# Attention value products gathered behind the two-bank score groups, and a hinted back edge for TensorE's loops

## The chip, the cores and the metric

One core of a Trainium2 chip. The metric is device time in microseconds for one execution of the whole program.

## The reference

One layer: attention with 16 heads of 16 features over 4096 rows of 256 features, a layer norm, an int8 feed-forward product and a second layer norm. Only the attention matters here. In short:

```python
query = qt_c + qt_r                      # [1, 16, 4096, 16]
key = kt_c + kt_r
value = heads(ct_kv @ Wu_v_w + Wu_v_b)
attn = jnp.einsum('bhqd,bhkd->bhqk', query, key) / scale
attn = jax.nn.softmax(attn, axis=-1)
out = jnp.einsum('bhqk,bhkd->bhqd', attn, value)
...
x = _layernorm(x + attention(x), axis=-1)
x = _layernorm(x + ffn(x), axis=-1)
```

## The kernel before

**Units.** A unit is one head with one half (2048) of the queries. There are 32 of them, done in 16 *pairs* (`PAIRS`), and a pair is one turn of the loop body on every engine. For a unit there are 32 tiles of 128 keys (`KT`) and 4 blocks of 512 queries (`QB`). A score block is a 128x512 product that fills one PSUM bank. Keys are split in two halves that lie in different partitions (rows 0 to 48 and 64 to 112), and blocks from different halves that stand next to each other run at the same time.

**Steps.** ScalarE makes the exponentials of 29 of the 32 key tiles, in 78 groups a pair (`NG`): even groups take four banks (0 to 3), odd ones two (4 and 5). Only group 38 is an even group of two. I call them exp 0 to exp 77. TensorE's body (`pair`) is one *step* for each group: wait for exp `s`, whose banks are then free; score group `s + 2` into them; at four steps in 13 one more score block in bank 6, for VectorE, which makes the exponentials of key tiles 15, 30 and 31 by bit operations and a polynomial (a *D block* below); and then the value products that stand in `VALUES[s]`. A D block waits until VectorE has read the one before it.

**Value products.** `values` multiplies the exponentials of one key tile with its values, for all four query blocks: four fp32 matmuls into four column strips of bank 7 (`OT`), which the trace shows as eight records. I call this a *set*. There are 64 in a pair, in a fixed order. After the last set of a unit VectorE copies bank 7 and normalises (`norm`, lines 770 to 786); the first set of the next unit waits for the copy. In VectorE's order the whole of `norm` stands ahead of its reading of the next D block.

**Where the sets stand.** `make_values` gives each set the first step, not before its exponentials are ready, that has no set yet. What is left over lands in step 77, so that step 77 has two sets.

**Loops.** TensorE runs pairs 0 to 8 in one loop, pair 9 written out (it also multiplies attention by the output weights, `project_step`), pairs 10 to 14 in a second loop, and pair 15 written out. So 12 of the 15 boundaries between pairs on TensorE are taken branches (8 in the first loop, 4 in the second), and at 3 of them (8 to 9, 9 to 10, 14 to 15) the code runs straight on. The other engines have loops of their own, which the change does not touch.

Of the kernel before, what the change touches and what calls it, by code (L numbers as in the profile page):

```python
# [19 lines left out]
PAIRS = NT // 2  # L20
# [33 lines left out]
NG = len(GROUPS)  # L54
# [15 lines left out]
def make_values():  # L70

    ready = []
    for g, (par, blocks) in enumerate(GROUPS):
        ready += [(g, par, kt) for kt, j in blocks if [b for b in ORDER if b[0] == kt][-1] == (kt, j)]
    for c in range(CYCLES):
        ready.append((STEPS_A_CYCLE * c + 6, c // len(BY_VECTOR), BY_VECTOR[c % len(BY_VECTOR)]))
    at = [[] for _ in range(NG)]
    earliest = 3
    for par in range(2):
        step = earliest  # L80
        for g, _, kt in sorted(r for r in ready if r[1] == par):
            step = max(step, g)
            at[min(step, NG - 1)].append((par, kt))
            step += 1
        earliest = step + 2
    return at


VALUES = make_values()
VALUE_ORDER = [v for at in VALUES for v in at]  # L90
assert [par for par, _ in VALUE_ORDER] == [0] * KT + [1] * KT
# [25 lines left out]
PROJECT_PAIR = 9  # L117
# [44 lines left out]
def build(nc, xT_d, x_d, w_d, bias_d, rows_d, tab_d, sel_d, ident_d, w8_d, out_d,  # L162
# [11 lines left out]
    with ctx:  # L174
# [323 lines left out]
        def attention_tensor(pe, a):  # L498
# [51 lines left out]
            def pair(i, more=True, project=False):  # L550
                for s in range(NG):
                    c, at = divmod(s, STEPS_A_CYCLE)

                    pe.wait_ge(a.exp, NG * i + s + 1)
                    if s + 2 < NG:
                        scores(s + 2)
                    elif more:
                        scores(s + 2 - NG)
                    if at in BLOCK_STEPS and (more or c + AHEAD < CYCLES):
                        n = QB * c + BLOCK_STEPS.index(at)  # L560
                        if project and n and (n - 1) % 3 == 0:
                            pe.wait_ge(a.added, (n - 1) // 3 + 1)
                        cycle_block(i, c, BLOCK_STEPS.index(at))
                    if project and at - 1 in BLOCK_STEPS:
                        n = QB * c + BLOCK_STEPS.index(at - 1)
                        if n % 3 == 0:
                            if n == 0:
                                pe.wait_ge(a.heads[0], 16 * 2)
                                pe.wait_ge(a.yb, KT)
                            project_step(n // 3)  # L570
                    for par, kt in VALUES[s]:
                        values(i, par, kt)
# [10 lines left out]
                    block(n, 0, kt, j)  # L583

            bias_out()
            with pe.Fori(0, PROJECT_PAIR) as i:
                pair(i)
            pair(PROJECT_PAIR, project=True)
            with pe.Fori(PROJECT_PAIR + 1, PAIRS - 1) as i:
                pair(i)  # L590
            pair(PAIRS - 1, more=False)

        def bias_out():

            for k in range(2):
                last = nc.tensor.matmul(PS[:, OT * CH:OT * CH + D], bv_wide[:, k, :],
                                        w[:, W_O + k * D:W_O + (k + 1) * D], start=k == 0, stop=k == 1)
            last.then_inc(s_bo, 1)
# [411 lines left out]
        def _(pe):  # L1010
# [64 lines left out]
            pe.wait_ge(s_dve, DONE - STEPS)  # L1075
            lengths("k", 0, 0)
            make_values(0, 8, (0, 0, 0, 0, 1, 2, 3, 4))

            pe.wait_ge(s_dve, DONE - STEPS + 5)
            pe.wait_ge(s_ev, E0 + 8)  # L1080
            lengths("k", 1, 4)

            pe.wait_ge(s_dve, DONE + 1)
            make_values(8, 12, (8, 8, 8, 8))

            pe.wait_ge(s_dve, DONE + 2)
# [13 lines left out]
            pe.wait_ge(s_sums, 1)  # L1100

            attention_tensor(pe, fast)


# [588 lines left out]
```

## Time and profile before

| what | value |
|---|---|
| device time, median of 3 runs | 2161.41 us (2157.86 to 2163.83) |
| profiled execution: its own time | 2160.25 us |
| profiled execution: its span | 2158.4 us |
| TensorE matmul busy | 1889.0 us (88%) |
| ScalarE busy | 1819.0 us (84%) |
| VectorE busy | 1612.8 us (75%) |
| mean granted TensorE clock | 0.958 |

The busy time is that of the whole span. Busy time of TensorE's weight loads is kept apart and overlaps with the matmuls. The clock is given as a share of full speed (2.4 GHz).

### The profile page before, as it was taken

How to read it: one execution, taken by the hardware profiler on the slowest of the kernel's cores; microseconds unless marked ns; L12 is line 12 of the kernel's file. 1: busy time of each engine (PE TensorE's matmuls, PEld its weight loads, DVE VectorE, ACT ScalarE, POOL GpSimd, SP SyncE). 2: the span in 40 equal slices, each digit the busy share in tenths (PEclk: the TensorE clock that was granted, in tenths of full speed). 3: DMA queues.
4: the chain of work that ended last, by engine and by line, in shares of the span. 5: the costliest groups of instructions: out<-in, count | busy, mean ns of one | idle time of the engine just before them, and what ended most of it. 6: DMA issues, size and time to landing. Idle time of an engine off the chain costs nothing.

```text
span 2158.4 us, 35517 instructions
## 1 busy us (share of the span) xinstructions
PE 1889.0 (88%) x13009; PEld 430.8 (20%) x13009; DVE 1612.8 (75%) x1514; ACT 1819.0 (84%) x1418; POOL 166.8 (8%) x129
## 2 busy tenths in 40 slices
PE   8957989898998989898989899898989989899975
PEld 3431111111111111111111122111111111111134
DVE  3648878777777777787777767887897778777838
ACT  4445989898998989898989977899989989898955
POOL 5725200000000000000000000000030000000002
PEclk9987999999999999999999999999999999999997
DMA  5652111110011111111111101111110101111012
GB/s 184 205 184 85 23 24 23 24 21 18 14 19 22 23 24 23 24 23 24 23 29 49 19 12 23 23 23 24 23 23 11 21 17 23 24 23 23 3 38 79
DMA packets 165495, 81.87 MB, mean 38 GB/s; under 512 B 130204, under 2 KB 146716, under 8 KB 164856
## 3 DMA queue, kind: packets, MB, share of 16 engines
q1 hardware_dynamic: 164024, 78.11, 14.0%
q8 instruction: 139, 2.28, 0.5%
q10 hardware_dynamic: 1312, 1.32, 0.2%
q14 instruction: 20, 0.16, 0.0%
HBM read 48.83 MB, written 29.23 MB: 36 GB/s over the span
## 4 chain that ended last, share of the span: by engine, by line
PE 68%; ACT 15%; issue 8%; DVE 5%; DMA 1%; SPq 1%; ACTq 0%; POOL 0%; DVEq 0%; POOLq 0%
PE PS L539 39%; PE PS L502 24%; ACT arena L762 15%; PE PS L1017 4%; PE PS L604 1%; DVE bn L692 1%; DMA Qst<-parts_or_sums 1%; DVE arena L816 1%; DVE arena L793 0%; DVE arena L1621 0%; DVE arena L746 0%; SPq L429 0%; DVE arena L749 0%; DVE parts_or_sums L1439 0%; DMA arena<-xT_dram 0%
## 5 line engine op out<-in xcount | busy, mean ns | idle before, releaser
L762 ACT ACTIVATE arena<-PS 128x2048 f32<-128x2048 f32 (+1 forms) x1248 | 1712.5, 1443 | 211.6 <-PE PS L502 202.1
L539 PE MATMUL PS<-arena,Vh 128*32 128x512 f32 x8192 | 1106.6, 614 | 0.5 <-ACT arena L762 0.5
L502 PE MATMUL PS<-Qst,Kst 49*128 49x512 f16 x4096 | 722.1, 393 | 207.3 <-ACT arena L762 145.7
L816 DVE SCALAR_TENSOR_TENSOR arena<-arena 128x2048 f32<-128x2048 f32 x288 | 660.4, 2293 | 0.2
L793 DVE TENSOR_SCALAR arena<-PS 128x512 int32<-128x512 f32 x384 | 265.2, 691 | 409.6 <-PE PS L502 398.7
L502 PEld LDWEIGHTS PS<-Qst,Kst 49*128 49x128 f16 x4096 | 156.2, 94 | 1205.6 <-ACT arena L762 772.0
L539 PEld LDWEIGHTS PS<-arena,Vh 128*32 128x32 f32 x8192 | 163.8, 108 | 378.9 <-issue 377.1
L812 DVE SCALAR_TENSOR_TENSOR arena<-arena 128x2048 f32<-128x2048 f32 x96 | 220.5, 2297 | 0.0
L800 DVE TENSOR_SCALAR arena<-arena 128x2048 int32<-128x2048 int32 x96 | 118.7, 1237 | 9.5
L738 POOL TENSOR_TENSOR ctkv<-arena,rows 128x256 f32<-128x256 f32 x16 | 21.2, 1362 | 1343.0 <-DVE arena L719 1343.0
L802 DVE TENSOR_SCALAR arena<-arena 128x2048 int32<-128x2048 int32 x96 | 118.7, 1237 | 0.0
L1017 PE MATMUL PS<-arena,w 128*128 128x512 f32 x192 | 90.3, 619 | 10.8 <-DMA bias<-biases_dram 6.8
L1220 ACT ACTIVATE arena<-PS,bias 128x512 f32<-128x512 f32 x56 | 38.4, 687 | 42.9 <-PE PS L1017 36.4
L738 POOL TENSOR_TENSOR arena<-arena,rows 128x256 f32<-128x256 f32 x16 | 11.1, 728 | 504.7 <-ACT arena L724 504.7
L1017 PEld LDWEIGHTS PS<-arena,w 128*128 128x128 f32 x192 | 38.0, 199 | 59.7 <-issue 52.6
L734 POOL TENSOR_TENSOR arena<-arena,rows 128x256 f32<-128x256 f32 x32 | 46.6, 1493 | 38.8 <-DVE rows L1458 38.8
L1427 DVE TENSOR_TENSOR arena<-arena 128x512 f32<-128x512 f32 x16 | 17.3, 1086 | 42.7 <-POOL arena L1342 40.2
L770 DVE COPY parts_or_sums<-PS 128x512 f32<-128x512 f32 x32 | 22.1, 691 | 33.5 <-PE PS L539 33.2
L1339 POOL TENSOR_TENSOR arena<-arena 32x512 f32<-32x512 f32 x16 | 26.2, 1638 | 39.4 <-DMA arena<-arena 39.4
L1439 DVE TENSOR_TENSOR parts_or_sums<-arena,parts_or_sums 128x1024 f16<-128x1024 f32 x16 | 27.4, 1751 | 0.0
L1340 POOL TENSOR_TENSOR arena<-arena 32x512 f32<-32x512 f32 x16 | 26.6, 1663 | 0.0
L604 PE MATMUL PS<-w,ctkv 128*128 128x256 f32 x64 | 19.1, 450 | 6.5 <-DVE arena L793 6.5
(104 smaller groups left out, 491.8 us busy)
## 6 DMA issues: line engine op xcount, KB each, us to landing
Kst<-k_halves SPq DMA_DIRECT2D x64, 128.0 KB
Qst<-q_halves SPq DMA_DIRECT2D x64, 128.0 KB
Vh<-head_values SPq DMA_DIRECT2D x30, 256.0 KB, 6.8
arena<-xT_dram SPq DMA_DIRECT2D x8, 512.0 KB, 5.3
k_halves<-parts_or_sums SPq DMA_DIRECT2D x16, 256.0 KB, 2.4
k_whole<-arena SPq DMA_DIRECT2D x8, 512.0 KB, 3.4
q_halves<-parts_or_sums SPq DMA_DIRECT2D x16, 256.0 KB, 3.4
q_whole<-arena SPq DMA_DIRECT2D x8, 512.0 KB, 4.3
```

Source lines behind the costliest of these rows:

```text
L502: return nc.tensor.matmul(out, Kst[par][low:low + HK + 1, at:at + 128], Qst[par][low:low + HK + 1, j * CH:(j + 1) * CH], start=True, stop= ...
L539: last = nc.tensor.matmul(PS[32 * j:32 * j + 32, OT * CH:(OT + 1) * CH], Vh[par][:, kt, :], moving, start=kt == first, stop=kt == last_kt)
L604: last = nc.tensor.matmul(out, heads_out(t // TH, c, t % TH * 128, 128), w[:, W_O + c * D:W_O + (c + 1) * D], start=c == 0 and starts, sto ...
L734: nc.gpsimd.tensor_tensor(Y[:, t, :], Y[:, t, :], bo, ALU.add).then_inc(s, 1)
L762: nc.scalar.activation(P[:, at * CH:(at + k) * CH], bank(SLOT_BANKS[g % 2][0], k), ACT.Exp, scale=EXP_SCALE).then_inc(a.exp, 1)
L793: nc.vector.tensor_scalar(bits[:, j * CH:(j + 1) * CH].bitcast(int32), bank(D_BANK), LOWEST, TO_BITS, ALU.max, ALU.mult).then_inc(b_bits, 1)
L800: nc.vector.tensor_scalar(mantissa.bitcast(int32), bits.bitcast(int32), 0x007FFFFF, 0x3F800000, ALU.bitwise_and, ALU.bitwise_or).then_inc( ...
L802: nc.vector.tensor_scalar(power.bitcast(int32), bits.bitcast(int32), 0x7F800000, 0x40000000, ALU.bitwise_and, ALU.bitwise_xor).then_inc(b_ ...
L812: nc.vector.scalar_tensor_tensor(out=t, in0=mantissa, scalar=POLY[3], in1=mantissa, op0=ALU.add, op1=ALU.mult).then_inc(b_poly, 1)
L816: last = nc.vector.scalar_tensor_tensor(out=t, in0=t, scalar=POLY[3 - j], in1=power if j == 3 else mantissa, op0=ALU.add, op1=ALU.mult)
L1017: last = nc.tensor.matmul(bank(out_bank), l, r, start=k == 0, stop=k == len(lhsT) - 1)
L1220: nc.scalar.activation(dst[e], bank(e), ACT.Identity, bias=bs[e], scale=scales[e]).then_inc(s_ev, 1)
```

## The change

`make_values` moves each set on to the next odd step, and lets an odd step take two sets; the last step takes what is left. TensorE's two loops get a hint for their closing branch, which stands as an instruction of its own at the head of the body. The order of the sets, all products and all waits stay.

```diff
@@ -80,8 +80,9 @@
         step = earliest
         for g, _, kt in sorted(r for r in ready if r[1] == par):
             step = max(step, g)
+            while step < NG - 1 and (step % 2 == 0 or len(at[step]) == 2):
+                step += 1
             at[min(step, NG - 1)].append((par, kt))
-            step += 1
         earliest = step + 2
     return at
 
@@ -583,10 +584,10 @@
             bias_out()
-            with pe.Fori(0, PROJECT_PAIR) as i:
+            with nc.Fori(0, PROJECT_PAIR, engines=(pe.engine,), hint_back_edge=True) as i:
                 pair(i)
             pair(PROJECT_PAIR, project=True)
-            with pe.Fori(PROJECT_PAIR + 1, PAIRS - 1) as i:
+            with nc.Fori(PROJECT_PAIR + 1, PAIRS - 1, engines=(pe.engine,), hint_back_edge=True) as i:
                 pair(i)
```

On TensorE, the order of the instructions in steps 3 to 7 of a pair, before (L502 is a score block, L539 the matmuls of a set, L554 and L513 the register steps of the waits for an exp and for VectorE):

```order
L502 MATMUL PS<-Qst,Kst 128x512
L529 ISA
L530 ISA
L539 MATMUL PS<-arena,Vh 32x512 x4
L554 REGISTER_ALU
L502 MATMUL PS<-Qst,Kst 128x512 x4
L539 MATMUL PS<-arena,Vh 32x512 x4
L554 REGISTER_ALU
L502 MATMUL PS<-Qst,Kst 128x512 x2
L539 MATMUL PS<-arena,Vh 32x512 x4
L554 REGISTER_ALU
L502 MATMUL PS<-Qst,Kst 128x512 x4
```

The same place after the change (all line numbers are one higher):

```order
L503 MATMUL PS<-Qst,Kst 128x512
L530 ISA
L531 ISA
L540 MATMUL PS<-arena,Vh 32x512 x8
L555 REGISTER_ALU
L503 MATMUL PS<-Qst,Kst 128x512 x4
L555 REGISTER_ALU
L503 MATMUL PS<-Qst,Kst 128x512 x2
L540 MATMUL PS<-arena,Vh 32x512 x8
L555 REGISTER_ALU
L503 MATMUL PS<-Qst,Kst 128x512 x4
```

The D block of step 3 has two sets behind it in place of one, and the four-bank scores of step 4 have none.

On TensorE, the end of a pair (steps 75 to 77) and the closing branch, before:

```order
L502 MATMUL PS<-Qst,Kst 128x512 x2
L554 REGISTER_ALU
L502 MATMUL PS<-Qst,Kst 128x512 x4
L539 MATMUL PS<-arena,Vh 32x512 x4
L554 REGISTER_ALU
L502 MATMUL PS<-Qst,Kst 128x512 x2
L539 MATMUL PS<-arena,Vh 32x512 x8
L586 REGISTER_ALU
L586 COMPARE_AND_BRANCH
```

After:

```order
L503 MATMUL PS<-Qst,Kst 128x512 x2
L540 MATMUL PS<-arena,Vh 32x512 x4
L555 REGISTER_ALU
L503 MATMUL PS<-Qst,Kst 128x512 x4
L555 REGISTER_ALU
L503 MATMUL PS<-Qst,Kst 128x512 x2
L540 MATMUL PS<-arena,Vh 32x512 x12
L587 REGISTER_ALU
L587 COMPARE_AND_BRANCH
```

Step 76 loses its set, and step 77 has three. The hint stands at the other end of the body, ahead of step 0:

```order
L587 UNCONDITIONAL_BRANCH
L587 BRANCH_PREFETCH_HINT
L587 ISA
L503 MATMUL PS<-Qst,Kst 128x512 x4
L514 ISA
L503 MATMUL PS<-Qst,Kst 128x512
```

In a pair, 63 steps had a set before; 35 have one after: 27 with two, 7 with one, and step 77 with three. The last set of the pair's first unit stands in step 39 (before: 38).

## Rows read from the trace of the kernel before

**Rows 1.** The page: busy time by engine, and the costliest groups
```profile
PE 1889.0 (88%) x13009; PEld 430.8 (20%) x13009; DVE 1612.8 (75%) x1514; ACT 1819.0 (84%) x1418; POOL 166.8 (8%) x129
...
L762 ACT ACTIVATE arena<-PS 128x2048 f32<-128x2048 f32 (+1 forms) x1248 | 1712.5, 1443 | 211.6 <-PE PS L502 202.1
...
L502 PE MATMUL PS<-Qst,Kst 49*128 49x512 f16 x4096 | 722.1, 393 | 207.3 <-ACT arena L762 145.7
```

**Rows 2.** Timeline, middle of a pair: start us, us, instructions [idle before]
```profile
599.85 1.87 ACT L762 ACTIVATE arena<-PS 128x2048 f32<-128x2048 f32 x1
601.61 1.03 ACT L762 ACTIVATE arena<-PS 128x1024 f32<-128x1024 f32 x1
...
602.06 0.61 PE L502 MATMUL PS<-Qst,Kst 49*128 49x512 f16 x4
602.60 1.07 PE L539 MATMUL PS<-arena,Vh 128*32 128x512 f32 x8
603.60 0.39 PE L502 MATMUL PS<-Qst,Kst 49*128 49x512 f16 x2
603.91 1.07 PE L539 MATMUL PS<-arena,Vh 128*32 128x512 f32 x8
604.91 0.82 PE L502 MATMUL PS<-Qst,Kst 49*128 49x512 f16 x5
```

**Rows 3.** Timeline, boundary of pairs 14 and 15, without a branch
```profile
1955.00 5.48 ACT L762 ACTIVATE arena<-PS 128x2048 f32<-128x2048 f32 x4 [0.27 <-PE PS L502]
1958.78 1.92 PE L539 MATMUL PS<-arena,Vh 128*32 128x512 f32 x16
1960.64 1.04 PE L502 MATMUL PS<-Qst,Kst 49*128 49x512 f16 x7
1960.77 0.69 DVE L770 COPY parts_or_sums<-PS 128x512 f32<-128x512 f32 x1 [0.46 <-PE PS L539]
1961.36 5.48 ACT L762 ACTIVATE arena<-PS 128x2048 f32<-128x2048 f32 x4 [0.89 <-PE PS L502]
1963.30 0.60 PE L502 MATMUL PS<-Qst,Kst 49*128 49x512 f16 x4 [1.62 <-ACT arena L762]
1965.30 0.60 PE L502 MATMUL PS<-Qst,Kst 49*128 49x512 f16 x1 [0.70 <-DVE arena L793]
1965.83 1.93 PE L539 MATMUL PS<-arena,Vh 128*32 128x512 f32 x8
1968.77 1.88 ACT L762 ACTIVATE arena<-PS 128x2048 f32<-128x2048 f32 x1 [1.93 <-PE PS L502]
1979.31 5.64 ACT L762 ACTIVATE arena<-PS 128x2048 f32<-128x2048 f32 x4 [0.20 <-PE PS L502]
```

**Rows 4.** Timeline, boundaries with the taken branch
```profile
534.48 1.37 PE L502 MATMUL PS<-Qst,Kst 49*128 49x512 f16 x7 [1.93 <-issue]
...
643.66 5.48 ACT L762 ACTIVATE arena<-PS 128x2048 f32<-128x2048 f32 x4 [0.27 <-PE PS L502]
651.73 1.04 PE L502 MATMUL PS<-Qst,Kst 49*128 49x512 f16 x7 [2.36 <-issue]
667.70 4.73 ACT L762 ACTIVATE arena<-PS 128x2048 f32<-128x2048 f32 x3 [0.20 <-PE PS L502]
...
760.42 5.48 ACT L762 ACTIVATE arena<-PS 128x2048 f32<-128x2048 f32 x4 [0.27 <-PE PS L502]
785.69 4.73 ACT L762 ACTIVATE arena<-PS 128x2048 f32<-128x2048 f32 x3 [0.20 <-PE PS L502]
...
886.73 1.89 PE L502 MATMUL PS<-Qst,Kst 49*128 49x512 f16 x7 [2.59 <-issue]
```

**Rows 5.** Stretches at the first and last boundary: us, busy time by engine, clock, DMA share, GB/s
```profile
301.00:305.00 4.00, 2.81 (x12) 0.51 (x15) 3.38 (x3) 3.70 (x3) 0.00 (x0) 0.50 0.35 89
...
1960.50:1964.50 4.00, 2.07 (x17) 0.51 (x13) 3.33 (x7) 3.14 (x3) 0.00 (x0) 1.00 0.22 73
1965.50:1971.50 6.00, 6.00 (x27) 0.84 (x30) 4.74 (x3) 3.54 (x4) 0.00 (x0) 0.50 0.62 95
```

## The prediction

> **What bounds the kernel now.** I read the page first. ScalarE and TensorE are both near 85% busy, and in the attention each waits for the other: the exponentials had 211.6 us of idle time ahead of them, nearly all ended by score blocks, and the score blocks had 207.3 us, most of it ended by the exponentials [rows 1]. So neither engine's sum is the limit. What counts is the ring: exp `s` frees its banks, scores `s + 2` fill them, exp `s + 2` can start.
>
> Then the timeline of a pair's middle. A four-bank exp is followed by the next after 1.76 us (601.61 - 599.85), and is itself 1.87 us long; a two-bank one is 1.03 us long [rows 2]. Four exps in a row take 5.48 us, of which the last two take 1.76 + 1.03 = 2.79, so an undisturbed double step takes ScalarE 2.69 us and the two-bank exp 0.93 of it [rows 2, 3]. TensorE: four-bank scores hold it for 0.54 us before the next set starts (602.06 to 602.60), two-bank ones 0.31, and a lone D block adds 0.21 (five blocks take 0.82, four 0.61), and a set 1.00 before the next scores (602.60 to 603.60) [rows 2].
>
> Then the boundary of two pairs, with z the start of exp 76. With the taken branch, TensorE stands still for 2.36 us on nothing the trace shows but issue (1.93 to 2.59 us at the 11 boundaries where it is named so) [rows 4]. From z to the start of exp 12 of the next pair it is 24.04 us (643.66 to 667.70) in one case and 25.27 in another (760.42 to 785.69) [rows 4]. Undisturbed, these 14 groups would be seven double steps, 7 x 2.69 = 18.8. From exp 12 on to the next exp 76 it is 92.72 us (667.70 to 760.42) [rows 4], against 31 x 1.76 + 33 x 0.93 = 85.3 undisturbed. So a pair loses about 5.2 to 6.4 us at its boundary and 7.4 us inside.
>
> The view that matters most is the boundary *without* a branch [rows 3]. There TensorE resumes at once (1960.64), and ScalarE waits only 0.89 us. But z to exp 12 is 24.31 us (1955.00 to 1979.31), as long as with the branch. VectorE can begin `norm` only at 1960.77, and reads the D block of step 0 only behind it; so the D block of step 3 waits until 1965.30, 4.53 us later, with the set and the four-bank scores of step 4 queued behind it, and ScalarE starves 1.93 us before exp 6 [rows 3]. TensorE, which had idled 1.62 us and then 0.70 us, is moreover at a granted clock of 0.50, the lower level of 1.2 GHz, over 1965.5 to 1971.5, after 1.00 up to 1964.5 (it fell at each of the 15 boundaries, the first of them at 301) [rows 5]; a set takes 1.93 us there [rows 3] in place of 1.07 [rows 2]. With the branch, these waits lie under the standstill.
>
> **The change, part by part.**
>
> *1. Sets by two.* Two sets back to back take 1.86 us until the next scores (1958.78 to 1960.64) [rows 3] where two apart take 2.00, so the second costs 0.87. Counting what is spared around the moved scores too: TensorE's double step with one set in each step is 0.54 + 1.00 + 0.31 + 1.00 = 2.85; with both sets behind the two-bank scores it is 0.43 (scores run straight on) + 0.31 + 1.86 = 2.60, or 0.25 less. In a pair 63 - 35 = 28 such changes go.
>
> What is it worth? Four-bank scores now wait for both sets, and these for the two-bank exp. The ring is: end of a two-bank exp, 0.05 until scores start, 0.31 of scores, 1.86 of sets, 0.65 from the start of four-bank scores to their exp, 1.76 to the next two-bank exp, 1.03 of it: 5.66 us for two double steps, 2.83 each. (0.05: I take the smallest wait that fits; 0.65 is 602.06 plus 0.61 plus hand-over.) Before, it was TensorE's own 2.85. So 0.02 is gained where 0.25 is spared: TensorE gets idle time, ScalarE little. D blocks in even steps (half of 24) become hidden behind the wait for the exp; those in odd steps still cost 0.22. Where double steps have fewer than two sets ScalarE is the limit in both versions.
>
> Laid out step by step with these durations from exp 12 to exp 76, the losses of ScalarE are, before: 4 x 0.14, 8 x 0.35, 7 x 0.24 and 1.54 around the two-bank groups 38 and 39, sum 6.6 (the trace has 7.4); after: 8 x 0.27, 4 x 0.22, 4 x 0.48, 3 x 0.05 and 1.44, sum 6.6. So inside a pair I take **0.0**. By averages (27 double steps with two sets; D blocks cost 0.62 x 0.22 each before, 0.31 x 0.22 after) it would be 27 x (2.99 - 2.90) = 2.4 us a pair less, or 39 us in all; that bounds it below.
>
> The last set of the pair's first unit moves from step 38 to 39, so `norm` and the D block of step 42 come about 1.2 us later. Nothing hangs on that block at once: steps 42 and 43 have no sets now. I take 0.
>
> *2. Three sets in step 77.* From z: exp 77 ends at 2.79, scores by 3.15, three sets 1.00 + 0.87 + 0.87 = 2.74, next scores at 5.9 (before, without a branch: 1960.64 - 1955.00 = 5.64 [rows 3]). So `norm` and all behind it come 0.25 us later.
>
> *3. The hint.* It takes away at most the standstill of 2.36 us [rows 4]; how much, no row shows: from 0 to all of it. I take all but a few tenths, since the target is known a whole pair ahead; the hint itself is one instruction in a step where TensorE then waits 1.62 us for ScalarE [rows 3]. A gap g of up to 0.5 us costs nothing, as the D block of step 3 is later anyway.
>
> The Trainium skill (Runtime: NRT & Kernel Launch, Instruction fetch mechanics) says that a taken branch to code outside the fetched pages stalls for the fetch. The trace agrees so far as the standstill stands at 12 branches and not at the straight boundaries.
>
> *4. The boundary then.* It becomes that of [rows 3], with three sets. From z: exp 2 at 5.9 + 0.65 = 6.55; D block of step 3 at 10.30 + 0.2 = 10.5 (1965.30 - 1955.00 = 10.30 [rows 3]); two sets from 10.8; scores of step 4 at 12.7, exp 6 at 13.35, 1.4 later than ScalarE could; exp 8 without loss at 16.05; exp 10 at 19.0; exp 12 at **21.7**. That holds at full clock. If the clock falls there as in [rows 5], two sets take 1.7 us more, scores 0.4, and exp 8 and exp 10 come late as well: exp 12 at **24.5**. Against the mean of the two branch cases, 24.65, a boundary gains 2.9 or 0.2.
>
> Does the clock fall? It fell at all 15 boundaries before, but at 12 of them after the standstill that goes now. Of the three straight ones, the one in [rows 3] had the idle times that I expect here (1.62 and 0.70), and there it fell. So neither end is excluded, and I take half: 1.4 us for each of 12 boundaries. The three straight ones stay.
>
> **Sum.** 12 x 1.4 = 17 us off 2160.25, the profiled execution's own time (span 2158.4 and 1.85 around it; 1.2 below the median of the runs): 2143 us.
>
> **The rivals.**
>
> *A, likeliest (0.48): the standstill goes and the clock holds at some or all boundaries.* 2118 (12 x 2.9 and some at the straight ones) to 2153; 2143 in the middle.
>
> *B (0.24): the standstill goes, nothing is gained.* `norm`, the D block of step 3 and the fallen clock take it all back, as in [rows 3]. 12 x 0.2: 2154 to 2162. For it: z to exp 12 without a branch equals that with one. Against it: the one sample.
>
> *C (0.10): the hint does nothing.* Then TensorE resumes at 8.07 from z as before (651.73 - 643.66 [rows 4]), the third set partly under the fetch, but step 3 has two sets at the low clock: 0.3 to 1.0 us more at 12 boundaries, 2164 to 2172.
>
> *D, slower (0.10): the second set of a step costs more than 0.87.* The 1.86 us stands in one kind of place only, step 77. If the second set cost 1.00, the ring would be 5.79 for two double steps: 27 x 0.065 = 1.8 us a pair, 28 us in all, and with A's 17 that is 2171. From 0.08 us more on a second set it outweighs A.
>
> *E (0.08): TensorE's sum does count.* If the scores of an even step could start well before they are needed, 28 x 0.25 = 7 us a pair would go, up to the 7.4 that a pair loses inside: 16 x 7 = 112 us, 2048. Against it: the ring of 5.66 us. The Trainium skill (TensorEngine Tiling (Array Packing), Key Properties) says that a change of tiling mode drains TensorE, which is what each change between scores (row tiles) and sets (column strips) is; by it alone the change would be worth this rival's time. The trace agrees with a cost, 0.25 us by the rows above.
>
> **The numbers.** Faster by over 0.3% (about what a measurement here tells from no change) means below 2155: A nearly whole and E, some of D's small end: 0.57. Within 0.3%: B and the edges of A and C, 0.27. Slower: 0.16. The range 2116 to 2166 takes A, B and a part of C, about 8 in 10.
>
> **What the profile after should show.** The "issue" gap before the scores of step 0 below 0.5 us at 12 boundaries (C wrong); ScalarE waiting about 1.1 us at exp 2; TensorE waiting for VectorE at step 3's D block; z to exp 12 between 21.7 and 24.5, and the clock low at fewer than 15 boundaries (A) or at all (B). Inside a pair, exp 12 to exp 76 at 92 to 93 us (E: below 88; D: above 94), with waits of about 0.27 us ahead of every second four-bank exp, and 16 records of a set pair in 1.92 us. TensorE's busy time falls while its waits for ScalarE grow. The prediction is wrong if the time inside a pair changes by over 1 us, or if the clock behaves alike at all boundaries.

## The result, and the profile after

The changed kernel takes 2239.16 us (median of 4 runs, 2237.22 to 2241.12) against 2162.03 us beside it: a ratio of 1.036, 95% interval 1.0341 to 1.0378. It is slower by 77 us where 17 to 19 us of gain were forecast. Two executions in what follows, one of e7 (3469.74 us) and one of the kernel before beside e5 to e8 (3475.03 us), ran in a slow state of the chip and count in no ratio.

The page of the kernel after, with the rows that answer to [rows 1], and the queue of instruction fetches:

```profile
PE 1920.4 (86%) x13009; PEld 500.5 (22%) x13009; DVE 1609.7 (72%) x1514; ACT 1813.0 (81%) x1418; POOL 166.8 (7%) x129
...
q8 instruction: 31, 0.51, 0.1%
...
L763 ACT ACTIVATE arena<-PS 128x2048 f32<-128x2048 f32 (+1 forms) x1248 | 1706.6, 1442 | 297.4 <-PE PS L503 294.6
...
L503 PE MATMUL PS<-Qst,Kst 49*128 49x512 f16 x4096 | 712.5, 402 | 255.2 <-ACT arena L763 199.0
```

ScalarE's idle time ahead of the exponentials has grown from 211.6 to 297.4 us, by 85.8; with the 5.9 us less that the exponentials themselves take (1712.5 to 1706.6) that is 80 of the 81 us by which the span grew (2158.4 to 2239.3). TensorE's idle time ahead of the scores grew from 207.3 to 255.2 us. The sets are the same work, and TensorE is busy 31 us longer with it: it ran slower. The mean granted clock over the span fell from 0.958 to 0.914.

The boundary of two pairs in the timeline after, with z, the start of exp 76, at 664.09:

```profile
664.09 5.48 ACT L763 ACTIVATE arena<-PS 128x2048 f32<-128x2048 f32 x4 [0.26 <-PE PS L503]
...
667.26 2.78 PE L540 MATMUL PS<-arena,Vh 128*32 128x512 f32 x24
...
669.97 1.04 PE L503 MATMUL PS<-Qst,Kst 49*128 49x512 f16 x7
...
670.70 5.48 ACT L763 ACTIVATE arena<-PS 128x2048 f32<-128x2048 f32 x4 [1.13 <-PE PS L503]
...
674.98 0.60 PE L503 MATMUL PS<-Qst,Kst 49*128 49x512 f16 x1 [1.05 <-DVE arena L794]
675.52 3.64 PE L540 MATMUL PS<-arena,Vh 128*32 128x512 f32 x16
...
680.16 2.79 ACT L763 ACTIVATE arena<-PS 128x2048 f32<-128x2048 f32 x2 [3.99 <-PE PS L503]
...
688.64 1.89 ACT L763 ACTIVATE arena<-PS 128x2048 f32<-128x2048 f32 x1
...
786.97 5.48 ACT L763 ACTIVATE arena<-PS 128x2048 f32<-128x2048 f32 x4 [0.26 <-PE PS L503]
```

The standstill of [rows 4] is gone: the scores of step 0 follow the three sets at once (669.97). The D block of step 3 waits 1.05 us for VectorE, its two sets take 3.64 us at the low clock, and ScalarE starves 3.99 us before exp 6. From z to exp 12 (688.64, read in a narrower stretch, which is why it stands alone) it is 24.55 us, against 24.04 and 25.27 in [rows 4]. So the boundary cost what it did before: added over all 15 boundaries of the two traces, z to exp 12 is 372.5 us before and 372.5 after.

The loss is inside the pair. The next exp 76 begins at 786.97, so exp 12 to exp 76 takes 98.33 us where it took 92.72 [rows 4]. Added over the 16 pairs it is 1579 us in place of 1500. The place around steps 41 to 45 in the timeline after (at 615.38 step 42 has brought no set, step 43 none, and step 44 begins):

```profile
610.94 1.92 PE L540 MATMUL PS<-arena,Vh 128*32 128x512 f32 x16
612.80 0.61 PE L503 MATMUL PS<-Qst,Kst 49*128 49x512 f16 x4
613.45 5.48 ACT L763 ACTIVATE arena<-PS 128x2048 f32<-128x2048 f32 x4 [0.19 <-PE PS L503]
613.62 0.60 PE L503 MATMUL PS<-Qst,Kst 49*128 49x512 f16 x3 [0.22 <-DVE arena L794]
615.38 0.63 PE L503 MATMUL PS<-Qst,Kst 49*128 49x512 f16 x4 [1.15 <-ACT arena L763]
616.29 1.04 PE L503 MATMUL PS<-Qst,Kst 49*128 49x512 f16 x3 [0.29 <-ACT arena L763]
617.26 3.64 PE L540 MATMUL PS<-arena,Vh 128*32 128x512 f32 x16
...
621.91 2.79 ACT L763 ACTIVATE arena<-PS 128x2048 f32<-128x2048 f32 x2 [2.98 <-PE PS L503]
```

Two sets take 3.64 us there and 1.92 before it. Between 612.80 and 617.26 TensorE has only scores, and waits for ScalarE in between. The idle times behind steps 17 and 67 are of the same kind (1.47 us, then 0.31; and 1.84):

```profile
576.44 0.60 PE L503 MATMUL PS<-Qst,Kst 49*128 49x512 f16 x4 [1.47 <-ACT arena L763]
...
653.02 1.57 PE L503 MATMUL PS<-Qst,Kst 49*128 49x512 f16 x7 [1.84 <-ACT arena L763]
```

The stretches of the same trace, behind the odd steps 17, 43 and 67, which have no set, and at the boundary (columns as in [rows 5]):

```profile
577.90:581.00 3.10, 3.10 (x17) 0.58 (x16) 2.89 (x2) 2.09 (x2) 0.00 (x0) 0.56 0.00 0
617.00:621.90 4.90, 4.90 (x23) 0.88 (x22) 4.36 (x3) 1.93 (x2) 0.00 (x0) 0.50 0.49 60
654.00:656.50 2.50, 2.50 (x15) 0.63 (x18) 2.29 (x2) 2.50 (x2) 0.00 (x0) 0.50 0.00 0
675.00:680.00 5.00, 5.00 (x23) 0.95 (x23) 4.92 (x3) 1.17 (x2) 0.00 (x0) 0.50 0.70 96
```

TensorE is at or near the low level of 1.2 GHz at four places in a pair, where it was at one. ScalarE's waits behind them, in every pair of the first loop: 2.05 us (before exp 22), 2.98 us (exp 48), 1.56 us (exp 72). Each is the first exp whose scores stand behind the slow sets.

### The profile page after: what moved, and what is told of

It reads as the page before. It is cut to its first block, busy times and chain, and to the rows that moved or that the text cites. A ratio compares the mean times of both kernels' runs of the same rounds, so it can differ in the third digit from the quotient of the medians.

```text
span 2239.3 us, 35532 instructions
## 1 busy us (share of the span) xinstructions
PE 1920.4 (86%) x13009; PEld 500.5 (22%) x13009; DVE 1609.7 (72%) x1514; ACT 1813.0 (81%) x1418; POOL 166.8 (7%) x129
## 4 chain that ended last, share of the span: by engine, by line
PE 52%; issue 21%; ACT 14%; DVE 9%; DMA 1%; SPq 1%; ACTq 1%; POOL 0%; DVEq 0%; POOLq 0%
PE PS L540 31%; PE PS L503 16%; ACT arena L763 13%; PE PS L1018 4%; PE PS L605 1%; DVE arena L794 1%; DVE parts_or_sums L778 1%; DVE parts_or_sums L773 1%; DVE parts_or_sums L771 1%; DVE bn L693 1%; DMA Qst<-parts_or_sums 1%; DVE arena L1622 0%; DVE arena L817 0%; ACTq L757 0%; DVE sum_inv L776 0%
## 5 line engine op out<-in xcount | busy, mean ns | idle before, releaser
L763 ACT ACTIVATE arena<-PS 128x2048 f32<-128x2048 f32 (+1 forms) x1248 | 1706.6, 1442 | 297.4 <-PE PS L503 294.6
L540 PE MATMUL PS<-arena,Vh 128*32 128x512 f32 x8192 | 1083.2, 645 | 1.6 <-ACT arena L763 1.6
L503 PE MATMUL PS<-Qst,Kst 49*128 49x512 f16 x4096 | 712.5, 402 | 255.2 <-ACT arena L763 199.0
L503 PEld LDWEIGHTS PS<-Qst,Kst 49*128 49x128 f16 x4096 | 168.9, 95 | 1079.8 <-ACT arena L763 895.3
L540 PEld LDWEIGHTS PS<-arena,Vh 128*32 128x32 f32 x8192 | 219.5, 115 | 515.0 <-issue 509.3
```

The costliest lines, as they stand in the source:

```text
L503: return nc.tensor.matmul(out, Kst[par][low:low + HK + 1, at:at + 128], Qst[par][low:low + HK + 1, j * CH:(j + 1) * CH], start=True, stop= ...
L540: last = nc.tensor.matmul(PS[32 * j:32 * j + 32, OT * CH:(OT + 1) * CH], Vh[par][:, kt, :], moving, start=kt == first, stop=kt == last_kt)
L763: nc.scalar.activation(P[:, at * CH:(at + k) * CH], bank(SLOT_BANKS[g % 2][0], k), ACT.Exp, scale=EXP_SCALE).then_inc(a.exp, 1)
```

## The experiments

Each ratio is against the kernel before, run beside that experiment.

Theory 1, formed from these rows: sets by two leave stretches without any set, longest where an odd step is empty; TensorE's clock falls there, and the two sets behind the stretch then run at half speed, with the four-bank scores, and so ScalarE, behind them. The rivals: the hint disturbs TensorE (theory 2), or the ring through two sets is long at any clock (theory 3).

**e1: the hint alone.** The kernel before with the loops of the change:

```diff
-            with pe.Fori(0, PROJECT_PAIR) as i:
+            with nc.Fori(0, PROJECT_PAIR, engines=(pe.engine,), hint_back_edge=True) as i:
```

> The hint alone, sets where they stood before. Theory 1 (the loss of the change is the low clock in stretches of a pair in which TensorE has no sets; the branch's standstill only covered a wait for VectorE): 2150 to 2165 us, the clock low once a pair, z to exp 12 about 24.3 us at every boundary as at the straight one, and 92 to 93 us from exp 12 to exp 76. Theory 2 (the hint itself disturbs TensorE's instruction supply and costs what was lost): 2200 to 2240 us. If the clock holds at some boundaries once the standstill is gone: 2115 to 2150.

2141.63 us, ratio 0.9921 (0.9904 to 0.9937), so about 17 us faster. Theory 2 falls. The boundary in its timeline, with z at 640.91:

```profile
640.91 5.48 ACT L762 ACTIVATE arena<-PS 128x2048 f32<-128x2048 f32 x4 [0.27 <-PE PS L502]
...
646.56 1.04 PE L502 MATMUL PS<-Qst,Kst 49*128 49x512 f16 x7
...
651.57 0.39 PE L502 MATMUL PS<-Qst,Kst 49*128 49x512 f16 x1 [1.05 <-DVE arena L793]
...
654.32 1.88 ACT L762 ACTIVATE arena<-PS 128x2048 f32<-128x2048 f32 x1 [1.56 <-PE PS L502]
...
661.12 2.79 ACT L762 ACTIVATE arena<-PS 128x2048 f32<-128x2048 f32 x2 [0.27 <-PE PS L502]
664.11 5.64 ACT L762 ACTIVATE arena<-PS 128x2048 f32<-128x2048 f32 x4 [0.20 <-PE PS L502]
...
756.83 5.48 ACT L762 ACTIVATE arena<-PS 128x2048 f32<-128x2048 f32 x4 [0.27 <-PE PS L502]
```

z to exp 12 is 23.20 us, 0.8 to 2.1 below the two of [rows 4]. Exp 12 to exp 76 is 92.72 us, the same to the hundredth as before. My expectation of about 24.3 at every boundary missed: the standstill of 2.4 us is covered by the wait for VectorE only in part, and the clock is low for a shorter time at eight of the twelve hinted boundaries (before: at two). Added up, the hinted boundaries are 15 us shorter. Another 3 us come from the straight boundary of pairs 14 and 15, which the hint does not touch: the clock held there this time (z to exp 12 is 21.25 us, 24.31 in [rows 3]).

**e2: the sets by two alone**, loops closed as before:

```diff
-            with nc.Fori(0, PROJECT_PAIR, engines=(pe.engine,), hint_back_edge=True) as i:
+            with pe.Fori(0, PROJECT_PAIR) as i:
```

> The sets by two alone, loops closed as before. Theory 1: 2235 to 2255 us, the clock low four times a pair, at the boundary and behind the odd steps without a set (17, 43, 67). Theory 2: back at about 2160. The branch's standstill should be there again, under 2.6 us, shorter if the third set of step 77 hides a part of the fetch.

2223.92 us, ratio 1.0308 (1.0291 to 1.0326), mean clock 0.933. So the loss comes with the sets. The time lies below the range that I gave, and 15 us below the whole change, though the standstill is back. The low clock fell into fewer places: its share of the span, (1 - clock) x 2, is 0.134, or 298 us, against 0.172, or 385 us. The trace splits the difference to the whole change: without the hint the 15 boundaries are 14 us longer (387 us in all), and the 16 insides 33 us shorter (1546 us). The wait of about 2 us before exp 22 is there in every pair, but the one before exp 48 is over 1 us in only 6 of the 16. So of the 80 us that the insides lost in the whole change, 47 come with the sets alone and 33 only with sets and hint together. Why the places differ was not tried; see below.

**e3: TensorE kept busy at the three empty steps.** The whole change, and in steps 17, 43 and 67 the scores of groups 19, 45 and 69 are made five times over, with the same result:

```diff
+REPEATS = {19: 5, 45: 5, 69: 5}
...
-                for k, (kt, j) in enumerate(blocks):
+                for k, (kt, j) in list(enumerate(blocks)) * REPEATS.get(g, 1):
```

> The whole change, with TensorE kept busy in steps 17, 43 and 67 by repeating their two-bank scores four more times (0.86 us each, the same values written again; nothing waits for it that has not 1.3 us to spare). Theory 1: the clock stays at full level inside a pair, exp 12 to exp 76 falls from 98.3 to 92 to 94 us, and the time to 2150 to 2175. Theory 3 (the ring through two sets is longer than laid out, whatever the clock does): no change from 2239, or slower.

2155.82 us, ratio 0.9981 (0.9972 to 0.9991). More matmuls, and 83 us less. Exp 12 to exp 76 is 92.56 us, within what was expected and 5.77 less than in the whole change:

```profile
663.48 1.89 ACT L766 ACTIVATE arena<-PS 128x2048 f32<-128x2048 f32 x1
...
756.04 1.88 ACT L766 ACTIVATE arena<-PS 128x2048 f32<-128x2048 f32 x1 [0.18 <-PE PS L506]
```

The waits before exps 22, 48 and 72, added over all pairs but 9, fall from 90 to 16 us, so most of the 83 us is gained at the three places. Theory 3 falls. The same place, steps 41 to 45, in its timeline, the answer to the rows of after above:

```profile
590.86 1.92 PE L543 MATMUL PS<-arena,Vh 128*32 128x512 f32 x16
592.72 0.61 PE L506 MATMUL PS<-Qst,Kst 49*128 49x512 f16 x4
...
593.54 1.47 PE L506 MATMUL PS<-Qst,Kst 49*128 49x512 f16 x11 [0.22 <-DVE arena L797]
595.30 0.61 PE L506 MATMUL PS<-Qst,Kst 49*128 49x512 f16 x4 [0.29 <-ACT arena L766]
596.21 0.60 PE L506 MATMUL PS<-Qst,Kst 49*128 49x512 f16 x3 [0.31 <-ACT arena L766]
596.75 1.92 PE L543 MATMUL PS<-arena,Vh 128*32 128x512 f32 x16
...
599.25 1.88 ACT L766 ACTIVATE arena<-PS 128x2048 f32<-128x2048 f32 x1 [0.41 <-PE PS L506]
```

Eight more score blocks (x11 in place of x3) fill 0.86 us of the idle 1.15. Nothing up to the scores of step 45 starts earlier (596.21 is 3.49 us behind 592.72, as 616.29 is behind 612.80). From there on the clock tells: these scores take 0.60 us in place of 1.04, the two sets 1.92 in place of 3.64, and ScalarE waits 0.41 us in place of 2.98. The stretch 592 to 598 of this trace has the full clock:

```profile
592.00:598.00 6.00, 5.18 (x42) 1.65 (x38) 5.74 (x7) 5.81 (x6) 0.00 (x0) 1.00 0.62 103
```

**e4: no empty odd step.** The whole change, with one set moved into each of the steps 17, 43 and 67 from the step two before:

```diff
+    for s in range(5, NG, 2):
+        if not at[s] and len(at[s - 2]) == 2:
+            at[s].append(at[s - 2].pop())
     return at
```

> The whole change, but no odd step of a unit without a set: one set each moves from steps 15, 41 and 65 to 17, 43 and 67. The work is that of the change. Theory 1: the stretches without sets are halved, the clock stays at full level inside a pair, 2150 to 2175 us. Theory 3: 2225 to 2240, as there are still 24 steps with two sets.

2146.58 us, ratio 0.9946 (0.993 to 0.9963): three sets of 64 a pair, moved by two steps, are worth 93 us. This is theory 1 with no work added. It is a little below the range I gave. In its timeline, z is at 636.12, exp 6 at 651.98, exp 10 at 657.73 and the next z at 752.21 (its rows and those of e1 above both show an exp 10):

```profile
636.12 5.48 ACT L766 ACTIVATE arena<-PS 128x2048 f32<-128x2048 f32 x4 [0.18 <-PE PS L506]
...
651.98 5.48 ACT L766 ACTIVATE arena<-PS 128x2048 f32<-128x2048 f32 x4 [3.42 <-PE PS L506]
657.73 5.48 ACT L766 ACTIVATE arena<-PS 128x2048 f32<-128x2048 f32 x4 [0.27 <-PE PS L506]
...
752.21 5.48 ACT L766 ACTIVATE arena<-PS 128x2048 f32<-128x2048 f32 x4 [0.18 <-PE PS L506]
```

z to exp 10 takes 21.61 us (e1: 661.12 - 640.91 = 20.21), and exp 10 to exp 76 takes 94.48 (e1: 756.83 - 661.12 = 95.71). So from exp 10 on, sets by two gain 1.2 us once the clock holds there, and this boundary gives back 1.4 (part of it by the clock, which is low for longer here than at that boundary of e1): exp 6 waits 3.42 us, with two sets behind the D block at the low level (columns as in [rows 5]).

```profile
647.00:651.50 4.50, 4.48 (x19) 0.83 (x21) 4.50 (x3) 1.56 (x2) 0.00 (x0) 0.50 0.75 111
```

**e5: the D blocks one step later.** The hint, sets one by one, and

```diff
-BLOCK_STEPS = (0, 3, 6, 9)
+BLOCK_STEPS = (0, 4, 7, 10)
...
+                    if par == 0:
+                        pe.wait_ge(s_bo2, 1)
                     pe.wait_ge(a.vh[par], 16 * (i + 1))
```

> The hint, sets where they stood before, and the D blocks one step later: steps 0, 4, 7 and 10 of 13 in place of 0, 3, 6 and 9 (with one wait more a pair, for the output bias, that is always over). Theory 1 says that with the hint the boundary hangs on the D block of step 3, which waits 1.05 us for VectorE's norm with a set and the scores of exp 6 behind it. In step 4 that wait is over: ScalarE's wait before exp 6 falls from 1.4 to 2.3 us to under 0.5, and the time from 2142 to 2108 to 2128. If the boundary hangs on the low clock alone, the time stays at 2135 to 2145.

(The wait for `s_bo2`, the output bias, is always over.) 2116.94 us, ratio 0.9797 (0.9779 to 0.9814), 25 us below e1. Two boundaries of its timeline. At the first, with z at 631.71, the set of step 3 runs at once and exp 6 waits only 0.22 us, but the clock falls, exp 8 waits 1.72, and z to exp 12 is 23.49, no shorter than in e1. At the second, with z at 747.71, the clock holds:

```profile
641.24 1.13 PE L541 MATMUL PS<-arena,Vh 128*32 128x512 f32 x8
...
643.77 1.88 ACT L764 ACTIVATE arena<-PS 128x2048 f32<-128x2048 f32 x1 [0.22 <-PE PS L502]
...
649.35 2.79 ACT L764 ACTIVATE arena<-PS 128x2048 f32<-128x2048 f32 x2 [1.72 <-PE PS L502]
...
747.71 1.88 ACT L764 ACTIVATE arena<-PS 128x2048 f32<-128x2048 f32 x1 [0.48 <-PE PS L502]
...
768.54 1.88 ACT L764 ACTIVATE arena<-PS 128x2048 f32<-128x2048 f32 x1
```

There z to exp 12 is 20.83 us. The clock holds at 5 of the 12 hinted boundaries, where it held at none in e1. So two things bound the boundary once the standstill was gone: `norm` with the D block behind it, and the low clock. e6 tells them apart.

**e6: the idle time of step 1 filled.** e1 with `REPEATS = {3: 5}`.

> The hint, sets where they stood before, and the two-bank scores of step 1 repeated four more times (0.86 us in TensorE's idle 1.62). If the low clock costs at the boundary beside the wait for VectorE, it holds more often and the time is 2120 to 2138; the wait for the D block of step 3 stays at about 1 us. If only that wait counts, 2140 to 2145.

2138.59 us, ratio 0.9904 (0.9886 to 0.9922): 3 us below e1, at the edge of what was expected, and not clear of it (the intervals overlap). The wait of 1.05 us for VectorE stays, as foretold. The clock holds at 3 of the 12 hinted boundaries, and one of these gives a price:

```profile
1100.26 5.48 ACT L765 ACTIVATE arena<-PS 128x2048 f32<-128x2048 f32 x4 [0.27 <-PE PS L505]
...
1121.86 1.88 ACT L765 ACTIVATE arena<-PS 128x2048 f32<-128x2048 f32 x1 [0.20 <-PE PS L505]
```

z to exp 12 is 21.60 us here, against 23.20 in e1 with the clock low for a part of it (23.19 at such boundaries of e6 itself), and 20.83 in e5. So the clock is worth 1.6 us at such a boundary, and the place of the D blocks 0.8 beyond that. The clock held at 3 boundaries with the fill, at 5 with the D blocks moved, and at 11 with both (e9).

**e7: sets by two with everything else mended.** e4 with the D blocks of e5 and the fill of e6.

> The whole change with no empty odd step (as in the fourth run), the D blocks one step later and the scores of step 1 repeated. If sets by two are worth anything once clock and D block are out of the way, this is faster than the fifth run by up to 2 us a pair; theory 1 says that it is not, since the ring through two sets is as long as TensorE's own double step was: 2105 to 2135, at or above the fifth run.

2119.75 us (2119.53 without the one of 3469.74), ratio 0.9807 (0.9786 to 0.9829). Not faster than e5. But not everything was mended: the D block of step 43 now waits for VectorE's `norm` in the middle of the pair, ScalarE waits 0.87 us or more before exp 46 in every pair of the first loop, which it does in none of e4's, and the clock fell inside 7 of the 15 ordinary pairs (all but 9).

**e8: one place filled.** The whole change with `REPEATS = {45: 5}`.

> The whole change, the repeated scores in step 43 alone. Theory 1: the place behind step 43 lost 2.98 us before one exp; it alone is mended, 16 times: 2239 - 16 x 2.5 to 3 = 2190 to 2200 us, with the waits of 2.05 us (behind step 17) and 1.56 us (behind step 67) left as they are or moved a little.

2193.9 us, ratio 1.0162 (1.0144 to 1.018). 45 us of the 83 come back by filling step 43 alone. The sum fits 16 x 2.98 = 48 us, but not all of it comes from this place. Added over all pairs but 9, the wait before exp 48 falls from 39 to 6.5 us; that before exp 72, whose place was not filled, falls too, from 21 to 12, and the 15 boundaries are 6 us shorter. So about 32 of the 45 us belong to the place.

**e9: the hint, the D blocks of e5, the fill of step 1, sets one by one.**

> The fifth run (hint, sets one by one, D blocks at steps 0, 4, 7, 10) with the scores of step 1 repeated four more times. The clock still fell at some boundaries in the fifth run; if it holds at more, 2105 to 2115 us. If the fillers gain as little as in the sixth run (3 us), 2112 to 2117. Against the seventh run (sets by two with the same fillers and D blocks, 2119.75) this shows what sets by two are worth: theory 1 says nothing, or a loss of up to 0.5 us a pair.

2110.2 us, ratio 0.9773 (0.9756 to 0.9789), mean clock 0.975. The fastest version. Against e7, which differs in the sets by two alone, it is 0.3% faster, with intervals that touch: sets by two gain nothing in this setting. That they could gain nothing in any is not shown: in e4 exp 12 to exp 76 is 91.80 us, in e9 92.51, and in e7, with the new wait before exp 46, 92.48 where the clock holds. In e9 the clock holds at 11 of the 12 hinted boundaries, with z to exp 12 between 20.62 and 20.84 us.

**e10: the D blocks at steps 0, 5, 8 and 11**, else as e5.

> The fifth run with the D blocks at steps 0, 5, 8 and 11. If the wait for VectorE at the boundary is over by step 4 already, this gains nothing more: 2110 to 2122 us. A gain of over 5 us would say that the D block of step 4 still holds something up.

2148.86 us, ratio 0.9952 (0.9937 to 0.9966). A miss: 32 us *slower* than e5, where nothing was expected. The waits of TensorE in its trace show a new one (columns: who waited for whom, us in total, times, longest):

```profile
PE PS L541 <- DVE parts_or_sums L772: 19.7, 16, 2.3
```

and ScalarE waits behind it, here before exp 44:

```profile
590.43 5.63 ACT L764 ACTIVATE arena<-PS 128x2048 f32<-128x2048 f32 x4 [1.63 <-PE PS L502]
```

The last D block of a cycle comes so late that VectorE's work on it holds up `norm`, and the first set of the pair's second unit waits 1.2 us for the copy of bank 7, once a pair. The clock then falls there too, inside 11 of the 15 ordinary pairs, where it fell inside none of them in e5. Exp 12 to exp 76 is 93.39 us in the pairs where it held and up to 94.69 where it fell, against 92.51 in e5; added over the 16 pairs that is 28.5 us of the 29.4 between the spans of the two traces.

## Why the prediction was wrong

**The step that failed is part 1, the laying out of the pair's inside.** It was done with the durations of [rows 2], at full clock, and the clock was asked about in part 4, at the boundary alone. Its own sentence, "TensorE gets idle time, ScalarE little", held the cause: the idle time was gathered where no set stands, up to 4.5 us from one pair of sets to the next (612.80 to 617.26). "Inside a pair I take 0.0" measured 5.6 us (92.72 to 98.33) in 12 of the 16 pairs, and 1.5 to 4.3 in the other four: 80 us in all. The boundaries, 372.5 us in both traces, gave nothing and took nothing, so this is the whole loss of the span, 81 us. Both signs that the prediction named of its being wrong came: the inside moved by over 1 us, and the clock was low at all 15 boundaries.

**At full clock the laying out was near.** e3, with the sets exactly where the change puts them, gives -0.2 us from exp 12 to exp 76 (92.72 to 92.56), where I took 0.0 and bounded it by -2.4. e4 gives -0.9 (91.80), or -1.2 from exp 10 on. A second set back to back costs 0.86 to 0.87 at any place: 16 records take 1.92 us and 24 take 2.78. Rival D (a dearer second set) falls. Rival E (TensorE's sum counts, 112 us) falls too: of the 25 x 0.25 = 6.2 us a pair that e4 spares on TensorE by the prediction's sum (38 steps with sets in place of 63), 1.2 reached ScalarE. So does the rule of the Trainium skill (TensorEngine Tiling (Array Packing), Key Properties) that a change of tiling mode drains TensorE, as a forecast of this change: the rows of before agree with a cost, 0.25 us for each double step that spares one round of changes (2.85 against 2.60), but it was not on the ring. No run tries that cost by itself.

**Three sets and the hint.** The standstill went as said, and ScalarE waited 1.13 us at exp 2 (forecast: 1.1). The D block of step 3 stood 10.89 us after z (forecast: 10.5), because VectorE's chain took a little longer. The two sets behind it took 3.64 us at the low clock, and z to exp 12 was 24.55 (the forecast's upper end was 24.5). The clock fell there at the boundary shown and at its two neighbours (the stretches below), and ScalarE waited 3.99 or 4.00 us before exp 6 at all eight boundaries of the first loop, so the half of 2.9 us that I took for the clock to hold was not there: rival B, for the boundary.

```profile
552.10:557.10 5.00, 4.99 (x23) 0.98 (x23) 4.95 (x3) 1.20 (x2) 0.00 (x0) 0.50 0.70 99
...
797.90:802.90 5.00, 5.00 (x23) 0.94 (x23) 4.90 (x3) 1.15 (x2) 0.00 (x0) 0.50 0.69 99
```

**The hint alone** gained 17 us (e1), the number that I gave for the whole, but by 1.2 us at a hinted boundary that still had one set behind the D block, in part because the low stretch was shorter, and with 3 us from a straight boundary. That the sum agrees is chance in part.

**What should have told.** [rows 3] and [rows 5] had shown the low level right behind idle waits of 1.62 and 0.70 us between scores. Laying out TensorE's idle time as well as ScalarE's would have shown such waits between score blocks in a stretch with few or no sets at three more places in each pair (1.47 and 0.31 us, 1.15 and 0.29, 1.84 in the trace after). It would have told where the clock can fall, and not how often it does: with the same order of work, e2 lost 47 us inside the pairs and the whole change 80. I had listed the empty steps (35 of 78 with a set) and not asked where they stood together.

## What to carry to other kernels

When TensorE is near but not on the limit, grouping its work saves switches and makes gaps; read where the gaps come together, since the clock can fall there and the work behind the gap then runs at half speed. Lay out the idle time of each engine, not only that of the one that sets the end, and price each gap at both clock levels. A wait that lies under another (here the taken branch over `norm`) is worth what is left of it when the other goes; find out what is next in line, and move that too: hint and D blocks together gave 44 us (e5), the hint alone 17.

## What the runs showed of the hardware

- **The hint does more than hide a fetch.** Packets on the instruction queue fell from 139 to 31 in the change, and stayed at 139 in e2, which has the same sets and no hint. That is 9 for each of the 12 taken branches; between 300 and 1000 us of the trace after, the queue moved nothing. The loop's body was then no longer fetched again in each turn. The Trainium skill (Runtime: NRT & Kernel Launch, Instruction fetch mechanics) speaks of a stall at a taken branch; that it goes with the hint is shown by e1 and after, where the scores of step 0 start with no gap.
- **Redundant matmuls can make a kernel faster**: 24 score blocks more in a pair, 83 us less (e3).
- **The number of low stretches depends on more than the order of the work.** After and e2 have the same order inside a pair; the low clock took 385 and 298 us. In e8, filling one place also changed how often the clock fell at another. In after each turn of the first loop has the same length (664.09 to 786.97 is 122.88 us) and the clock falls at the same places in each. What decides whether it falls at a given place was not tried, and stays open.
